# A graph network's gather loop: stores of gathered rows issued by ScalarE instead of SP

## The chip, the cores and the metric

One core of a Trainium2 chip. The metric is the time on the device of one execution, in microseconds (us). The kernel before takes 5740.17 us, the median of three runs (5734.01 to 5756.72).

## The reference, cut to what matters

Four layers of graph networks run one after the other on 6250 nodes of 128 features and 100,000 edges sorted by their target, each followed by a residual and a layer norm. The change lies in the second, a graph attention layer with four heads of 32:

```python
x_l = (x @ Wl + bl).reshape(n, H, C)
x_r = (x @ Wr + br).reshape(n, H, C)
e = (ea_f @ We).reshape(-1, H, C)
m = jax.nn.leaky_relu(x_l[src_f] + x_r[dst_f] + e, NEG_SLOPE)
alpha = jnp.einsum('ehc,hc->eh', m, att)
amax = jax.ops.segment_max(alpha, dst_f, num_segments=n)
aexp = jnp.exp(alpha - amax[dst_f])
asum = jax.ops.segment_sum(aexp, dst_f, num_segments=n)
alpha = aexp / (asum[dst_f] + 1e-16)
out = jax.ops.segment_sum(x_l[src_f] * alpha[..., None], dst_f, num_segments=n)
```

The sum over edges in the other layers is done as a product with a dense matrix of counts (adjacency) of 6272 x 6400 fp16 numbers, kept in HBM. The fourth layer needs that matrix transposed.

## The kernel before

The program is written for each engine by hand, with semaphores: every engine has its own list of instructions, which it does in order, and a wait holds up all that stands behind it on that engine. The stages are: building the matrix of counts by scattered writes, three dense layers, the attention layer (scores, maxima, sums), a dense layer pair, and a last pair that uses the transposed matrix.

**The stage of scores.** 832 visits (a visit is 128 edges of one tile of nodes) are done in 104 groups of U = 8, in 26 rounds of RING = 4. A group g uses slot j = g mod 4 of `msg`, a ring of four buffers of 128 x 8 x 128 fp32. What happens to a group:

- ScalarE (L771) copies its eight columns of indices into `stage`, once DVE has reported group g-4 as done (`s_add`). This sets off the gather.
- GpSimd (L624, "POOL") waits for the staging and issues eight indirect DMAs, one for each visit. Each gathers 128 rows of `x_l` from HBM into `msg`, and `s_gath[j]` counts what has landed.
- DVE (L1383) makes one-hot matrices one group ahead, PE (L966) transposes them, ScalarE (L773) copies the result to `diag`, and PE (L972) multiplies it with the rows of `x_r`.
- DVE (L1396 to L1406) waits for the products and for the gather, and computes the scores in six operations. Then it waits for the store of the same group (`s_store[j]`) and reports the group as done.
- SP (L518) waits for the gather and stores `msg[:, j]` to `gathered` in HBM, 512 KB, from where the stage of sums reads it back later.

**The transposes.** Beside this SP makes the transposed matrix of counts, in 25 rounds of four pieces. A piece is a DMA transpose (L515) from `adj` in HBM into a slot of `turns` in SBUF, and a save of it (L509, function `save`) into `turned` in HBM. `s_turn[j]` and `s_saved[j]` count both. In a round SP does, for each j: wait for the save of the round before, issue the transpose, wait for the gather of the group, issue its store, wait for the transpose, issue its save. The 26th round has stores alone (L523). DVE waits for all saves only after the stage, ahead of its scans, and the last layers read `turned`.

Of the kernel before, what the change touches and what calls it, by code (L numbers as in the profile page):

```python
# [16 lines left out]
P = 128  # L17
U = 8
RING = 4
# [18 lines left out]
def build(nc, x, src, dst, edge_weight, W1, b1, W2, b2, W3, b3, gWl, gbl, gWr, gbr, gWe, gatt, gbias,  # L38
# [5 lines left out]
    CT = TILES + 1  # L44
# [4 lines left out]
    ROUNDS = GROUPS // RING  # L49
# [18 lines left out]
    with ctx:  # L68
# [6 lines left out]
        def sem(name):  # L75
            return ctx.enter_context(nc.semaphore(name))

        def dram(name, shape, dt=F32):
            return nc.dram_tensor(name, shape, dt, kind="Internal").ap()
# [7 lines left out]
        gathered = dram("gathered", (VISITS // U * P, U * D))  # L87
# [110 lines left out]
        s_gath = [sem(f"s_gath{j}") for j in range(RING)]  # L198
        s_store = [sem(f"s_store{j}") for j in range(RING)]
# [81 lines left out]
        msg = rows_of[:, :, :, 0:D]  # L281
# [64 lines left out]
        def go(name):  # L346
            return GO.index(name) + 1
# [84 lines left out]
        def _(sp):  # L432
# [73 lines left out]
            def save(i, j):  # L506
                a, z = PARTS[j % 2]
                sp.wait_ge(s_turn[j], i * 16 + 16)
                sp.dma_start(turned[bass.ds(i * (2 * P) + j // 2 * P, P), a * P:z * P], turns[:, j, 0:(z - a) * P]).then_inc(s_saved[j], 16)  # L509

            with sp.Fori(0, CT // 2) as i:
                for j in range(RING):
                    a, z = PARTS[j % 2]
                    sp.wait_ge(s_saved[j], i * 16 + 16)
                    sp.dma_start_transpose(turns[:, j, 0:(z - a) * P].rearrange("p (o c) -> p o c", o=1),  # L515
                                           adj[a * P:z * P, bass.ds(i * (2 * P) + j // 2 * P, P)]).then_inc(s_turn[j], 16)
                    sp.wait_ge(s_gath[j], i * (16 * U) + 16 * U)
                    sp.dma_start(gathered[bass.ds(i * (RING * P) + j * P, P), :].rearrange("p (u f) -> p u f", u=U), msg[:, j, :, :]).then_inc(s_store[j], 16)  # L518
                    save(i, j)
            with sp.Fori(CT // 2, ROUNDS) as i:  # L520
                for j in range(RING):
                    sp.wait_ge(s_gath[j], i * (16 * U) + 16 * U)
                    sp.dma_start(gathered[bass.ds(i * (RING * P) + j * P, P), :].rearrange("p (u f) -> p u f", u=U), msg[:, j, :, :]).then_inc(s_store[j], 16)  # L523
            sp.wait_ge(s_go, go("shifted"))

            def read_back(a, z):
# [131 lines left out]
        def _(act):  # L658
# [108 lines left out]
            with act.Fori(0, ROUNDS) as i:  # L767
                for j in range(RING):

                    act.wait_ge(s_add, i * (RING * U) + (U * (j - RING + 1) + ADD0))  # L770
                    act.copy(stage[:, j * U:(j + 1) * U], idxA[:, bass.ds(i * (RING * U) + j * U, U)]).then_inc(s_staged, 1)  # L771
                    act.wait_ge(s_oT, i * RING + (j + 1))
                    act.copy(diag[:, j % 2, :, :], pm[:, j % 2, :].rearrange("p (u f) -> p u f", f=P)).then_inc(s_oTc, 1)  # L773
            act.wait_ge(s_go, go("shifted"))
            act.activation(ext[:, :, 0:H], ext[:, :, 0:H], ACT.Exp).then_inc(s_exp, 1)
            with act.Fori(0, ROUNDS) as i:
# [859 lines left out]
```

## Time and profile before

| | |
|---|---|
| median of the runs | 5740.17 us (5734.01 to 5756.72) |
| profiled execution | 5702.34 us |
| its span | 5700.5 us |
| busy in the span | PE 58%, DVE 49%, POOL 36%, ACT 29% |
| stage of scores | from about 2350 to 3640 us of the span |

The span is the time from the first to the last instruction of that one execution. Shares of busy time are means over stages with different limits. In the trace "SPq" and "ACTq" are the instructions with which an engine issues DMAs, and they do not count as its busy time; "issue" is idle time for which the profile shows no releaser, and "remote" idle time that ended on a semaphore whose sender it does not show.

### The profile page before, as it was taken

What the parts mean: (1) busy time and instruction counts of PE and PEld (TensorE: products, weight loads), DVE (VectorE), ACT (ScalarE), POOL (GpSimd) and SP (SyncE); (2) the same over time, 40 slices, a digit from 0 to 9 for tenths busy, and PEclk for the clock granted to TensorE, in tenths of its full rate; (3) what the DMA queues carried; (4) which work ended last, traced back from release to release, by engine and by line L of the source; (5) the groups of instructions that cost most, each with busy time, mean ns of one, the idle gap of its engine ahead of it and who ended that gap; (6) DMA issues with size and microseconds to landing.
All of it is one profiled execution on the core that took longest, in us unless ns stands there. A gap on an engine that the chain in (4) does not pass through costs nothing.

```text
span 5700.5 us, 61044 instructions
## 1 busy us (share of the span) xinstructions
PE 3324.1 (58%) x19159; PEld 3100.7 (54%) x19160; DVE 2808.7 (49%) x3801; ACT 1675.3 (29%) x2774; POOL 2048.7 (36%) x1982
## 2 busy tenths in 40 slices
PE   1300000019999999544444444357479999689697
PEld 0300000019999999544333343246379789589597
DVE  8300000024454544677666677788954344544345
ACT  0000000005645455200000000023266356456265
POOL 2777666750000000377677777346300000200300
PEclk9999999999999999755555555579789999799798
DMA  9700000008858587499899899247368268478585
GB/s 356 275 1 16 1 1 1 1 12 278 257 183 276 175 275 227 126 228 220 215 216 214 215 221 222 62 122 214 92 205 277 84 208 277 151 244 285 180 283 183
DMA packets 887483, 1008.44 MB, mean 177 GB/s; under 512 B 391651, under 2 KB 651705, under 8 KB 887270
## 3 DMA queue, kind: packets, MB, share of 16 engines
q1 hardware_dynamic: 795778, 861.50, 51.6%
q0 software_dynamic: 56208, 63.97, 4.8%
q10 hardware_dynamic: 35284, 80.30, 3.6%
q8 instruction: 113, 1.85, 0.1%
q14 instruction: 100, 0.82, 0.1%
HBM read 692.09 MB, written 233.14 MB: 162 GB/s over the span
## 4 chain that ended last, share of the span: by engine, by line
PE 44%; another core or an unknown queue 23%; DVE 14%; issue 11%; POOL 3%; ACT 2%; DMA 2%; DVEq 1%; SPq 0%; ACTq 0%; POOLq 0%
PE banks L918 35%; PE banks L841 4%; POOL work L624 2%; PE banks L1000 2%; DVE Z L1397 1%; DVE big L1519 1%; DVE Z L1402 1%; PE banks L863 1%; ACT banks L779 1%; DVE big L1406 1%; DMA work<-tab,stage 1%; DVE Z L1404 1%; ACT X L668 1%; PE banks L966 1%
## 5 line engine op out<-in xcount | busy, mean ns | idle before, releaser
L918 PE MATMUL banks<-wides,rows 128*128 128x384 f32 (+2 forms) x11040 | 2028.5, 344 | 155.8 <-issue 88.6
L918 PEld LDWEIGHTS banks<-wides,rows 128*128 128x128 f32 x11040 | 1949.4, 189 | 229.1 <-issue 94.3
L624 POOL DMA_INDIRECT work<-tab,stage x832 | 902.8, 1085 | 1483.0 <-ACT stage L771 1232.2
L1265 DVE CAST wides<-big 128x768 fp32r<-128x768 f16 (+3 forms) x1429 | 811.1, 569 | 1176.7 <-PE banks L918 1072.3
L698 ACT CAST wides<-big 128x768 fp32r<-128x768 f16 (+2 forms) x1037 | 832.2, 804 | 677.9 <-PE banks L918 554.3
L598 POOL DMA_INDIRECT cells<-queue_i x784 | 787.0, 1004 | 311.9 <-issue 298.6
L972 PE MATMUL banks<-V,work 128*128 x1664 | 372.5, 414 | 378.6 <-ACT work L773 312.1
L972 PEld LDWEIGHTS banks<-V,work 128*128 128x128 f32 x1664 | 345.1, 316 | 415.9 <-issue 415.9
L650 POOL DMA_INDIRECT V<-tab,nodei x100 | 96.2, 962 | 1201.9 <-DMA tab<-X 879.8
L863 PE MATMUL banks<-work 128*128 128x50 f16 x784 | 92.1, 278 | 670.6 <-issue 600.5
L863 PEld LDWEIGHTS banks<-work 128*128 128x128 f16 x784 | 73.1, 149 | 689.5 <-issue 612.6
L773 ACT COPY work<-banks 128x1024 f32<-128x1024 f32 x104 | 105.3, 1012 | 1152.4 <-remote 542.5
L696 ACT ACTIVATE wides<-big 128x768 fp32r<-128x768 f16 (+1 forms) x392 | 342.5, 874 | 186.4 <-PE banks L918 186.4
L966 PE MATMUL banks<-ident,work 128*128 128x128 f32 x832 | 184.5, 395 | 331.4 <-DVE work L1383 259.4
L661 ACT ACT_TABLE_LOAD x1 | 1.3, 1283 | 1250.5 <-DVEq L1053 1250.5
L1193 DVE TENSOR_TENSOR work<-big 128x400 f16<-128x400 f16 x98 | 36.2, 369 | 668.7 <-remote 641.0
L966 PEld LDWEIGHTS banks<-ident,work 128*128 128x128 f32 x832 | 148.5, 206 | 356.6 <-DVE work L1383 279.3
L1396 DVE TENSOR_TENSOR Z<-banks,work 128x1024 f32<-128x1024 f32 x104 | 127.1, 1222 | 310.5 <-remote 167.0
L1000 PE MATMUL banks<-work 128*128 128x137 f32 x1664 | 226.6, 289 | 84.8 <-ACT banks L779 53.6
L1000 PEld LDWEIGHTS banks<-work 128*128 128x128 f32 x1664 | 206.3, 193 | 105.3 <-issue 105.3
L639 POOL TENSOR_TENSOR work<-work,big 128x1024 f32<-128x1024 f32 x104 | 199.9, 1922 | 0.0
L779 ACT COPY banks<-zeros 128x1233 f32<-128x1233 f32 x104 | 123.6, 1189 | 176.6 <-DVE big L1519 176.6
(300 smaller groups left out, 3229.1 us busy)
## 6 DMA issues: line engine op xcount, KB each, us to landing
big<-cells SPq DMA_DIRECT2D x490, 416.0 KB
big<-cells SPq DMA_DIRECT2D x441, 384.0 KB
big<-turned SPq DMA_DIRECT2D x300, 384.0 KB
gathered<-work SPq DMA_DIRECT2D x104, 512.0 KB
work<-gathered SPq DMA_DIRECT2D x104, 512.0 KB, 4.2
big<-turned SPq DMA_DIRECT2D x100, 416.0 KB
cells<-work ACTq DMA_DIRECT2D x98, 416.0 KB, 14.6
turned<-big SPq DMA_DIRECT2D x50, 800.0 KB
```

The costliest lines, as they stand in the source:

```text
L598: pool.indirect_dma_start(cells[:, :], bass.IndirectOffsetOnAxis(ap=queue_i[:, b % 2, u:u + 1].bitcast(U32), axis=0), queue_i[:, b % 2, PI ...
L624: pool.indirect_dma_start(msg[:, j, u, :], None, tab[0][:, :], bass.IndirectOffsetOnAxis(ap=stage[:, j * U + u:j * U + u + 1].bitcast(U32) ...
L639: pool.tensor_tensor(m, m, by_head, ALU.mult).then_inc(s_msgs, 1)
L696: act.activation(to, of, ACT.Copy, accum_out=degs[:, s, k - OTHER + 1, w:w + 1]).then_inc(s_widea, 1)
L698: act.copy(to, of).then_inc(s_widea, 1)
L841: last = pe.matmul(pm[:, b % 2, i * P:(i + 1) * P], lhsT, rhs, start=(n == 0), stop=(n == len(ab) - 1))
L863: last = pe.matmul(col_ps, ohl[:, h, :, u], ohh[:, h, :, u], start=False, stop=False, skip_group_check=True)
L918: last = pe.matmul(banks[:, 4 * (w % 2) + j, 0:(z - a) * P], rows2[:, s, part * D:(part + 1) * D], wides[:, q % QUEUE, (a - start) * P:(z ...
L966: last = pe.transpose(pm[:, j % 2, u * P:(u + 1) * P], oh[:, j % 2, u, :], ident[:, :])
L972: last = pe.matmul(ps[:, j % 2, u, :], diag[:, j % 2, u, :], Vf[:, bass.ds(t * P, P)], start=True, stop=True)
L1000: last = pe.matmul(gsums[j % 2][:, bass.ds(slot, GW)], oh[:, j % 2, u, :], rows_of[:, j, u, :], start=False, stop=False, skip_group_check= ...
L1265: dve.tensor_copy(wides[:, (2 * m + 1) % QUEUE, 0:(z - a) * P], halves[:, m % HALVES, a * P:z * P]).then_inc(s_wided, 1)
```

## The change

ScalarE waits, after its copy to `diag`, for the gather of the same group and issues the store of its rows. In SP's loop the store and its wait are gone, and so is the loop for the 26th round. SP issues the transpose of piece j before it waits for transpose j-1 and saves it, so that two can be in flight; the last of a round is saved before the next round begins.

```diff
--- before.py
+++ after.py
@@ -514,13 +514,9 @@
                     sp.wait_ge(s_saved[j], i * 16 + 16)
                     sp.dma_start_transpose(turns[:, j, 0:(z - a) * P].rearrange("p (o c) -> p o c", o=1),
                                            adj[a * P:z * P, bass.ds(i * (2 * P) + j // 2 * P, P)]).then_inc(s_turn[j], 16)
-                    sp.wait_ge(s_gath[j], i * (16 * U) + 16 * U)
-                    sp.dma_start(gathered[bass.ds(i * (RING * P) + j * P, P), :].rearrange("p (u f) -> p u f", u=U), msg[:, j, :, :]).then_inc(s_store[j], 16)
-                    save(i, j)
-            with sp.Fori(CT // 2, ROUNDS) as i:
-                for j in range(RING):
-                    sp.wait_ge(s_gath[j], i * (16 * U) + 16 * U)
-                    sp.dma_start(gathered[bass.ds(i * (RING * P) + j * P, P), :].rearrange("p (u f) -> p u f", u=U), msg[:, j, :, :]).then_inc(s_store[j], 16)
+                    if j:
+                        save(i, j - 1)
+                save(i, RING - 1)
             sp.wait_ge(s_go, go("shifted"))
 
             def read_back(a, z):
@@ -771,6 +767,8 @@
                     act.copy(stage[:, j * U:(j + 1) * U], idxA[:, bass.ds(i * (RING * U) + j * U, U)]).then_inc(s_staged, 1)
                     act.wait_ge(s_oT, i * RING + (j + 1))
                     act.copy(diag[:, j % 2, :, :], pm[:, j % 2, :].rearrange("p (u f) -> p u f", f=P)).then_inc(s_oTc, 1)
+                    act.wait_ge(s_gath[j], i * (16 * U) + 16 * U)
+                    act.dma_start(gathered[bass.ds(i * (RING * P) + j * P, P), :].rearrange("p (u f) -> p u f", u=U), msg[:, j, :, :]).then_inc(s_store[j], 16)
             act.wait_ge(s_go, go("shifted"))
             act.activation(ext[:, :, 0:H], ext[:, :, 0:H], ACT.Exp).then_inc(s_exp, 1)
             with act.Fori(0, ROUNDS) as i:
```

ScalarE, in the loop of the stage of scores, before (the numbers of the lines are those of each kernel; `s_oT` is PE's transposes, `s_add` DVE's report):

```order
L771 ISA [waits s_add]
L771 COPY stage<-idxA 128x8
L772 ISA
L773 COPY work<-banks 128x1024 [waits s_oT]
L770 REGISTER_ALU
L771 ISA [waits s_add]
L771 COPY stage<-idxA 128x8
```

The same place in the changed kernel:

```order
L767 ISA [waits s_add]
L767 COPY stage<-idxA 128x8
L768 ISA
L769 COPY work<-banks 128x1024 [waits s_oT]
L770 ISA
L771 ISA [waits s_gath0]
L771 DMA gathered<-work 1024x1x128
L766 REGISTER_ALU
L767 ISA [waits s_add]
L767 COPY stage<-idxA 128x8
```

The wait for the gather and the store stand between the copy of one group and the staging of the next.

SP, the start of its loop in the same stage, before:

```order
L515 DMA_TRANSPOSE big<-cells 128x1x3200
L517 ISA
L518 ISA [waits s_gath0]
L518 DMA gathered<-work 1024x1x128
L509 ISA [waits s_turn0]
L509 DMA turned<-big 128x3200
L515 ISA [waits s_saved1]
L515 DMA_TRANSPOSE big<-cells 128x1x3072
```

And in the changed kernel:

```order
L515 DMA_TRANSPOSE big<-cells 128x1x3200
L515 ISA [waits s_saved1]
L515 DMA_TRANSPOSE big<-cells 128x1x3072
L509 ISA [waits s_turn0]
L509 DMA turned<-big 128x3200
L515 ISA [waits s_saved2]
L515 DMA_TRANSPOSE big<-cells 128x1x3200
```

The second transpose has moved ahead of the wait for the first, and nothing of the gathers is left.

## Rows read from the trace of the kernel before

**Rows 1.** The page: span, busy time of each engine, and the group of the gathers

```profile
span 5700.5 us, 61044 instructions
...
PE 3324.1 (58%) x19159; PEld 3100.7 (54%) x19160; DVE 2808.7 (49%) x3801; ACT 1675.3 (29%) x2774; POOL 2048.7 (36%) x1982
...
L624 POOL DMA_INDIRECT work<-tab,stage x832 | 902.8, 1085 | 1483.0 <-ACT stage L771 1232.2
```

**Rows 2.** Busy time by stretch: the stage of scores, and a piece near its end

```profile
core 0: us, PE busy (x) PEld busy (x) DVE busy (x) ACT busy (x) POOL busy (x), PEclk, DMA share, GB/s
2350.00:3640.00 1290.00, 564.61 (x2566) 501.37 (x2564) 896.14 (x740) 116.58 (x208) 902.76 (x832) 0.58 0.88 212
3590.00:3622.00 32.00, 18.18 (x81) 16.08 (x80) 29.27 (x26) 4.51 (x6) 25.33 (x22) 0.55 0.28 77
```

**Rows 3.** L624: durations (min/median/max), first and last start; what its idle time waited for

```profile
L624 POOL DMA_INDIRECT work<-tab,stage x832: 939/951/1996, 2350.4 to 3622.7; - x167
...
  issue: 250.8, 791
...
POOL work L624 <- ACT stage L771: 1232.2, 41, 1112.2
```

**Rows 4.** Lines of DMA issues: the store from SP, and ScalarE's clearing stores (ns min/median/max)

```profile
L518 SPq DMA_DIRECT2D gathered<-work x100: 453/578/715, 2383.7 to 3580.1; - x100
...
L740 ACTq DMA_DIRECT2D cells<-work x245: 5/867/3243, 22.9 to 282.4; - x123
```

**Rows 5.** Timeline of SP at the start of the stage: start, duration, instruction

```profile
2380.35 2.77 SPq L515 DMA_TRANSPOSE big<-cells  x1
...
2386.94 4.87 SPq L515 DMA_TRANSPOSE big<-cells  x1
...
2395.88 4.47 SPq L515 DMA_TRANSPOSE big<-cells  x1
...
2403.94 5.91 SPq L515 DMA_TRANSPOSE big<-cells  x1
```

**Rows 6.** Timeline of all engines, 3000 to 3031 us: three groups' last issues and landings

```profile
3000.73 0.94 POOL L624 DMA_INDIRECT work<-tab,stage  x1 [0.31 <-issue]
...
3005.95 0.58 SPq L518 DMA_DIRECT2D gathered<-work  x1
...
3008.91 5.36 SPq L515 DMA_TRANSPOSE big<-cells  x1
...
3011.59 0.96 POOL L624 DMA_INDIRECT work<-tab,stage  x1 [0.30 <-issue]
...
3015.33 1.01 ACT L773 COPY work<-banks 128x1024 f32<-128x1024 f32 x1 [21.44 <-remote]
...
3016.24 0.20 ACT L771 COPY stage<-idxA 128x8 int32 x1
...
3017.23 1.60 POOL L624 DMA_INDIRECT work<-tab,stage  x1 [4.68 <-ACT stage L771]
...
3019.22 0.59 SPq L518 DMA_DIRECT2D gathered<-work  x1
...
3020.64 6.16 SPq L515 DMA_TRANSPOSE big<-cells  x1
...
3028.15 0.95 POOL L624 DMA_INDIRECT work<-tab,stage  x1 [0.30 <-issue]
...
3031.08 0.57 SPq L518 DMA_DIRECT2D gathered<-work  x1
```

**Rows 7.** Timeline, the last gather of the stage

```profile
3622.68 1.33 POOL L624 DMA_INDIRECT work<-tab,stage  x1 [0.30 <-issue]
3626.25 0.53 SPq L523 DMA_DIRECT2D gathered<-work  x1
```

**Rows 8.** Waits in the stage: who waited for whom, us in total, times, longest

```profile
ACT work L773 <- remote: 542.5, 31, 22.1
...
ACT work L773 <- PE banks L966: 414.7, 50, 20.5
```

## The prediction, made before the changed kernel had run

> **What bounds the stage now.** The profile's page comes first [rows 1]: no engine is near its span, GpSimd's gathers (L624) carry 902.8 us in 832 instructions, and the line of that group names ScalarE's staging of indices (L771) as what ended its idle time. The stretch from 2350 to 3640 us is the stage of scores, the only one in which the edit changes an instruction [rows 2]: POOL 902.8 and DVE 896.1 of 1290 us, PE 565, ACT only 117, and the 16 DMA engines 0.88 busy. In the undisturbed end of the stage, without transposes, the DMA share is 0.28.
>
> The lines on L624 then split POOL's time [rows 3]. Its first issue is at 2350.4 us and its last at 3622.7, so 104 groups of eight issues take 1272.3 us, 12.23 us each. One issue is 1.085 us on average, and the idle time before one is some 0.30 us of "issue" (250.8 us in 791 cases). Of the 1232.2 us of waiting for ACT, 1112.2 are one wait before the stage, so 120.0 us in 40 cases lie inside it. A group is 8 x 1.085 + 7 x 0.305 = 10.8 us of issuing. So **POOL issues almost without a break now**: 10.8 of 12.2 us. It can do so because ScalarE stages the indices of a group ahead of time: it waits for group g-4 and for PE's transposes of group g, but never for the gather itself. DVE's 896.1 us are 8.6 us per group: it is not the bound.
>
> **What the change removes.** SP loses 104 store issues of some 0.58 us [rows 4] and 104 waits for gathers. Its transposes lose those waits too: now one transpose at a time is issued, and the next one only after a store of gathered rows. Nobody in this stage waits for a transpose or for its save; their results are first needed after the stage. This part is worth nothing by itself, unless the freed DMA time brings the gathers home earlier. It also makes the transposes come denser. The first four transposes of the stage, before SP had gathers to wait for, are issued at 2380.35, 2386.94, 2395.88 and 2403.94 us [rows 5], 7.9 us apart on average. I take 8.5 us, since the end of each loop turn waits for its last transpose with nothing else in flight: 100 of them take 850 us, not the 1200 of now.
>
> **What it adds, on the critical path.** ScalarE now runs, per group: wait for group g-4, stage g, wait for PE, copy the diagonal matrix of g, **wait until gather g has landed, issue its store**, and only then stage g+1. POOL cannot start gather g+1 before it is staged. What stands behind the new wait is therefore the one instruction that POOL depends on, and POOL's run-ahead is gone: the loop is POOL issues 8, the last one lands, ScalarE issues the store, ScalarE stages, POOL issues again. Its terms:
>
> - The issuing, 10.8 us as now. Below that, with every issue at its 0.951 us median [rows 3], 9.7 us.
> - From the end of the eighth issue to the start of the instruction that waits for the landing. I read it where SP waits in the same way today. Three groups in a row give 3001.67 to 3005.95 = 4.28, 3012.55 to 3019.22 = 6.67 and 3029.10 to 3031.08 = 1.98 us [rows 6]. SP's own transpose had been issued by 3014.27 in the second and 3026.80 in the third, so SP was waiting. Their mean is 4.3. Without transposes, at the end, it is 3624.01 to 3626.25 = 2.2 us [rows 7].
> - ScalarE's issue of the store. SP takes 0.578 us for it, and ScalarE 0.867 for one of its clearing stores [rows 4]. The first is the same transfer, so 0.6. Register work adds 0.1.
> - Start of staging to POOL's first issue: 3016.24 to 3017.23 = 1.0 us [rows 6].
>
> The sum is 10.8 + 4.3 + 0.7 + 1.0 = **16.8 us per group while transposes run**, and 10.8 + 2.2 + 0.7 + 1.0 = **14.7 us after them**. In the first 850 us fit 51 groups (857 us), and the other 53 take 779 us: 1636 us against 1272, **364 us more**.
>
> What else could be late: PE's work and ScalarE's copies hang on the staging of their group as before, and both together are (565 + 117) / 104 = 6.6 us per group [rows 2], which fits beside a gather of 15 us or more. DVE (896.1 / 104 = 8.6 us a group) finishes a group that long after its gather has landed, before the next one lands, so it falls idle instead. It waits for the store of its own group, which ScalarE issues at once and which has those 8.6 us to land. The next stages are not touched. They start later by the whole amount, since the scan waits for the last group.
>
> The profiled execution took 5702.3 us for a span of 5700.5. The sum would make it 6066. The median of the runs shown is 38 us above the profiled one, so the forecast for the median is 5740 + 364 = **6104 us**.
>
> The bounds of the terms together: 9.7 + 1.98 + 0.7 + 1.0 = 13.4 us per group gives 1394, or 5862 us; 10.8 + 6.7 + 1.0 + 1.0 = 19.5 gives 2028, or 6496 us. The landing is the open term. I take the mean of its rows for the first part and the undisturbed one for the rest, as the transposes end early.
>
> **Where a rule and the rows part.** The gathers' landing moves between 2.0 and 6.7 us with what SP has in flight [rows 6, 7]. The Trainium skill, "DMA: Bandwidth & Descriptors", section "SWDGE vs HWDGE vs iDMA", says that GpSimd's and SP's descriptors sit in different queues of each DMA engine and that the engine takes turns between them. By that rule a gather would wait for little of a transpose, and the landing would stay near its short value throughout. That is the first rival; the 6.67 us speak against it.
>
> **Rivals.**
>
> 1. Landings stay short under the transposes: 14.7 us in all 104 groups, 1529 us, **5997 us**. For it speaks the row of 1.98 us; against it 4.28 and 6.67. Chance 0.08. With the issuing faster as well, at the lower bound: 5862 us, chance 0.03.
> 2. The denser transposes hold up every gather as long as the worst row: 10.8 + 6.7 + 0.7 + 1.0 = 19.2 us for 850 us are 44 groups (845 us), and 60 of 14.7 are 882: 1727 us, **6195 us**. For it speaks that a transpose or a save would nearly always be in flight. Chance 0.12.
> 3. The DMA engines are the bound, and what they move per stage stays: no change, **5740 us**. For it stands the share of 0.88. Against it, POOL issues its gathers all the same, with 120 us of idle time in the stage. It would need DMA queues so full that a break of 6 us in every group costs nothing. Chance 0.03. The Trainium skill says in "DMA: Bandwidth & Descriptors", section "Issuing engines are not separate DMA queues", that starting DMAs from another engine saves only the time of issuing them: by this rule the gain side is nil, and the trace agrees as far as SP's issue of 0.58 us goes.
> 4. **Faster.** ScalarE arrives at the new wait when the gather has already landed. Then the wait is free, staging is as early as now, and the earlier landing of stores (no longer behind a transpose and its save in SP's order) takes away POOL's waits of 120.0 us: **5620 us**. This decides at the point where the diagonal copy (L773) starts after the landing. In the rows it starts at 3015.33, and the store of the same group goes out at 3019.22 [rows 6]; read in the same way over the timeline, the copy starts before the store in all but 2 of the 104 groups. For it speaks that ScalarE idles for PE before that copy (414.7 us) and for others (542.5 us) [rows 8], so it is late often, but not that late. Chance 0.04.
>
> That ScalarE would not wait in this order is excluded by the listing of its instructions.
>
> **Chances.** The forecast has 0.70. Slower by over 0.5% (29 us, about what a measurement of this kernel can tell) are the forecast and rivals 1 and 2: 0.70 + 0.08 + 0.03 + 0.12 = 0.93. Within it 0.03, faster 0.04. The range leaves out rivals 3 and 4 and the low bound (0.10) and the far ends of the landing: 5950 (14.2 us per group, between the two lower sums) to 6270 (17.3 us in every group, as if the transposes disturbed to the end).
>
> **What would show it.** In the profile of the changed kernel: POOL's idle time before L624 put down to ScalarE in nearly all 104 groups, 4 to 6 us each, some 500 us in all beside the wait before the stage; ScalarE's store 2 to 7 us after the eighth issue and its staging within 1 us of it; transposes 8 to 9 us apart and over by some 3250 us; DVE idle for gathers in every group; a lower DMA share, and POOL's pitch near 17 us early and 15 us late. It is wrong if POOL's issues still follow each other over the bounds of groups, or if the pitch does not fall once the transposes are over.

## The result: 5.7% slower, and the profile after

The changed kernel takes **6067.74 us** (median of four runs, 6065.19 to 6069.82) against 5737.82 us before: 330 us more, a ratio of 1.0566 with a 95% interval of 1.0545 to 1.0587. The forecast was 6104 us, in a range of 5950 to 6270.

The page of the changed kernel, in the rows that answer to [rows 1], and its DMA queues (number of packets, MB, share of 16 engines):

```profile
span 6067.3 us, 61052 instructions
...
L620 POOL DMA_INDIRECT work<-tab,stage x832 | 883.5, 1062 | 1876.7 <-ACT stage L767 1646.0
...
q1 hardware_dynamic: 687618, 806.96, 44.2%
q10 hardware_dynamic: 143444, 134.83, 6.5%
```

The gathers are L620 now. Their issuing takes what it took (883.5 us, 902.8 before), and the idle time ahead of them has grown. The stores have moved from SP's queue (q1) to ScalarE's (q10). The 832 issues, and the waits in the stage (who waited for whom: total us, times, longest):

```profile
L620 POOL DMA_INDIRECT work<-tab,stage x832: 940/952/1992, 2377.5 to 3991.6; - x167
...
POOL work L620 <- ACT stage L767: 1646.0, 104, 1145.2
ACT stage L767 <- DMA work<-tab,stage: 1093.7, 77, 19.4
...
DVE Z L1394 <- DMA work<-tab,stage: 644.4, 103, 11.6
```

The stage, from the first issue to the last, lasts 3991.6 - 2377.5 = 1614 us; before it was 1272 [rows 3]. POOL waits for ScalarE in all 104 groups: 1646.0 - 1145.2 = 500.8 us inside the stage, where it was 120.0 in 40 cases. ScalarE in turn waits for gathers to land, and so does DVE, for 644.4 us; before, the profile puts 109 us of DVE's idle time in the stage down to gathers, and 167 us to no sender that it shows. The transposes, which SP now issues alone, and the stage cut where they end (SP's line first, then busy time by stretch, with the columns of [rows 2]):

```profile
L515 SPq DMA_TRANSPOSE big<-cells x100: 1452/5430/8637, 2410.0 to 3102.7; - x100
```

```profile
2378.00:3130.00 752.00, 247.54 (x1094) 219.13 (x1092) 372.85 (x305) 48.79 (x87) 365.22 (x345) 0.56 1.11 278
3280.00:3990.00 710.00, 277.14 (x1194) 244.93 (x1192) 423.82 (x350) 55.44 (x100) 424.99 (x400) 0.58 0.26 74
```

They are 7.0 us apart ((3102.7 - 2410.0) / 99), and the last is issued at 3102.7 us. POOL makes 345 issues in 752 us while they run, which is **17.4 us per group**, and 400 in 710 us afterwards, **14.2 us per group**. The DMA share is 1.11 in the first part and 0.26 in the second. Two turns of the loop, in the timeline of the changed kernel (start, duration, instruction, idle time before it): one among transposes, then one after them.

```profile
2997.26 0.94 POOL L620 DMA_INDIRECT work<-tab,stage  x1 [0.30 <-issue]
...
3002.78 0.55 ACTq L771 DMA_DIRECT2D gathered<-work  x1
3003.74 0.20 ACT L767 COPY stage<-idxA 128x8 int32 x1 [15.99 <-issue]
...
3004.72 1.17 POOL L620 DMA_INDIRECT work<-tab,stage  x1 [6.53 <-ACT stage L767]
```

```profile
3806.68 0.94 POOL L620 DMA_INDIRECT work<-tab,stage  x1 [0.30 <-issue]
...
3809.52 0.55 ACTq L771 DMA_DIRECT2D gathered<-work  x1
3810.25 0.20 ACT L767 COPY stage<-idxA 128x8 int32 x1 [13.07 <-DMA work<-tab,stage]
...
3811.23 1.41 POOL L620 DMA_INDIRECT work<-tab,stage  x1 [3.61 <-ACT stage L767]
```

The chain can be read off: the eighth issue ends (2998.20), the gather lands and ScalarE issues the store (2.78, so 4.58 us later), then stages (0.96 later), then POOL issues again (0.98 later). In the second turn the first step takes 3807.62 to 3809.52 = 1.90 us, the other two 0.73 and 0.98. Averaged over groups, the first step takes 5.0 us in the first 43 and 1.7 in the others, and the other two together 1.8 in both. Nothing else of the program moved: from the last gather to the end of the span it is 2077.8 us before and 2075.7 after. The stage begins at 2350.4 us in the one profile and at 2377.5 in the other, with the same code ahead of it; in the first four experiments it begins anywhere from 2351 to 2368. So the spans lie 367 us apart, the stages 342 and the medians 330.

### The profile page after: what moved, and what is told of

The parts are those of the page before. It is cut to its first block, busy times and chain, and to the rows that moved or that the text cites. A ratio compares the mean times of both kernels' runs of the same rounds, so it can differ in the third digit from the quotient of the medians.

```text
span 6067.3 us, 61052 instructions
## 1 busy us (share of the span) xinstructions
PE 3338.1 (55%) x19159; PEld 3112.8 (51%) x19160; DVE 2813.1 (46%) x3801; ACT 1675.2 (28%) x2774; POOL 2014.3 (33%) x1982
## 4 chain that ended last, share of the span: by engine, by line
PE 40%; another core or an unknown queue 16%; POOL 12%; issue 11%; DVE 9%; DMA 7%; ACT 2%; ACTq 1%; DVEq 0%; SPq 0%; POOLq 0%
PE banks L916 32%; POOL work L620 12%; DMA work<-tab,stage 6%; PE banks L839 4%; PE banks L998 1%; ACTq L771 1%; DVE big L1517 1%; DVE Z L1302 1%; ACT banks L777 1%; PE banks L861 1%; ACT X L664 1%; DVE V L1113 1%; PE banks L826 0%; PE banks L892 0%
## 5 line engine op out<-in xcount | busy, mean ns | idle before, releaser
L620 POOL DMA_INDIRECT work<-tab,stage x832 | 883.5, 1062 | 1876.7 <-ACT stage L767 1646.0
L594 POOL DMA_INDIRECT cells<-queue_i x784 | 771.3, 984 | 320.2 <-issue 308.1
L767 ACT COPY stage<-idxA 128x8 int32 x104 | 20.5, 197 | 1480.8 <-DMA work<-tab,stage 1093.7
L1394 DVE TENSOR_TENSOR Z<-banks,work 128x1024 f32<-128x1024 f32 x104 | 127.4, 1225 | 650.2 <-DMA work<-tab,stage 644.4
## 6 DMA issues: line engine op xcount, KB each, us to landing
cells<-work ACTq DMA_DIRECT2D x98, 416.0 KB, 14.7
```

The source lines that it names most:

```text
L594: pool.indirect_dma_start(cells[:, :], bass.IndirectOffsetOnAxis(ap=queue_i[:, b % 2, u:u + 1].bitcast(U32), axis=0), queue_i[:, b % 2, PI ...
L620: pool.indirect_dma_start(msg[:, j, u, :], None, tab[0][:, :], bass.IndirectOffsetOnAxis(ap=stage[:, j * U + u:j * U + u + 1].bitcast(U32) ...
```

## The experiments

All ran as one core's program, each compared with the kernel before on the same chip. The experiments ran on three chips, of two sorts: on that of experiments 1 to 4 before takes 5711 us, about as above; on that of 5 to 8 and on that of 9 to 12, 5164 to 5165 us. Ratios hold within a chip; the lengths of the stage (first to last issue of the gathers) are set side by side where the same kernel ran on both.

### The wait, the store, the two halves

**1. The wait alone.** The kernel before, with ScalarE waiting for the gather, and SP storing and transposing as before:

```diff
                     act.copy(diag[:, j % 2, :, :], pm[:, j % 2, :].rearrange("p (u f) -> p u f", f=P)).then_inc(s_oTc, 1)
+                    act.wait_ge(s_gath[j], i * (16 * U) + 16 * U)
```

> The kernel before, with one added wait: ScalarE waits for the gather of group g before it stages group g+1. SP still issues stores and transposes as before. Theory (the wait takes away POOL's run-ahead): per group 10.7 us of issuing, 3.5 to 5 us to the landing, 1.1 us of staging, no 0.6 us store issue: 15.3 to 16.8 us, a stage of 1590 to 1750 us, a time of 6040 to 6200 us. Rival A (the store's 104 DMA issues on ScalarE are what costs): within 1% of before, 5680 to 5800 us. Rival B (the denser transposes hold up the gathers): within 1% of before too, since the transposes keep their old pace.

Measured: 5845.42 us, a ratio of 1.023 (1.0196 to 1.0264). The wait by itself costs 2.3%, so both rivals fall as sole causes, but the time lies 195 us under the low end of what I expected. The stage lasts 1409 us, 13.5 us per group:

```profile
L624 POOL DMA_INDIRECT work<-tab,stage x832: 942/947/1962, 2363.4 to 3772.3; - x167
```

```profile
2996.34 0.59 SPq L518 DMA_DIRECT2D gathered<-work  x1
...
2997.12 0.51 SPq L509 DMA_DIRECT2D turned<-big  x1
...
2997.76 6.57 SPq L515 DMA_TRANSPOSE big<-cells  x1
...
3006.42 0.95 POOL L624 DMA_INDIRECT work<-tab,stage  x1 [0.30 <-issue]
...
3009.10 0.20 ACT L771 COPY stage<-idxA 128x8 int32 x1 [11.66 <-DMA work<-tab,stage]
```

The rows (SP's store, save and transpose; POOL's eighth issue; ScalarE's staging) show why. SP issues its whole share right after a landing and has issued the transpose by 3004.33; the last gather of the next group goes out at 3006.42 and meets little of it. It lands 1.73 us after its issue (3007.37 to 3009.10). Where POOL stands still until a landing, and the transfers of SP start at the same landing, the two keep out of each other's way. I had taken the landing from a kernel in which they do not.

**2. The store one group late.** The changed kernel, with ScalarE's wait and store for group g-1 behind the copy of group g (`store` is the same wait and store for a given group; round 0 is written out, since its first group has none in front):

```diff
-                    act.wait_ge(s_gath[j], i * (16 * U) + 16 * U)
-                    act.dma_start(gathered[bass.ds(i * (RING * P) + j * P, P), :].rearrange("p (u f) -> p u f", u=U), msg[:, j, :, :]).then_inc(s_store[j], 16)
+                    if j:
+                        store(i * (16 * U) + 16 * U, bass.ds(i * (RING * P) + (j - 1) * P, P), j - 1)
+                    else:
+                        store(i * (16 * U), bass.ds(i * (RING * P) - P, P), RING - 1)
```

> The changed kernel, with ScalarE's wait and store moved one group later: stage g, copy g, then wait for gather g-1 and store it. SP as changed (dense transposes, no stores). Theory: staging of g+1 waits only for the landing of g-1, which falls into POOL's issuing of g, so POOL issues without a break: 11.0 to 12.2 us per group, stage 1150 to 1270 us, time 5610 to 5740 us. Rival A (store issues on ScalarE cost): stays above 5950 us, for there are as many. Rival B (dense transposes cost): stays well above before in the first 700 us of the stage, a pitch of 15 us or more there. Rival C (the 16 DMA engines are the bound, at 0.88 busy before): no faster than before, 5700 to 5780 us, with DMA share near 1.

Measured: 5728.52 us, 1.0031 (1.0013 to 1.0049). ScalarE issues as many stores, SP's transposes run free as well (8.0 us apart), and nearly the whole loss is gone. So neither the number of stores on ScalarE nor the dense transposes cost much by themselves; they cost where POOL waits for what stands behind them. Busy time while the transposes run and after them:

```profile
2400.00:3190.00 790.00, 355.70 (x1520) 313.64 (x1520) 531.81 (x444) 73.37 (x127) 567.07 (x509) 0.57 1.17 281
3220.00:3640.00 420.00, 185.69 (x856) 164.57 (x855) 296.29 (x246) 41.08 (x70) 300.11 (x279) 0.60 0.32 88
```

509 issues in 790 us are 12.4 us per group, against 17.4 in the changed kernel under the same DMA share of 1.1 to 1.2. The hoped-for gain did not come: POOL still makes only 279 issues in the 420 us after the transposes, 12.0 us per group. The waits in that kernel's stage name one place:

```profile
DVE work L1398 <- DMA gathered<-work: 168.1, 54, 8.6
```

DVE waits for the store of its own group, which now goes out a group late. It is the smaller part, though: read group by group, POOL's 35 waits in the stage come to 124 us, and 77 us of them (19 waits) follow a copy to `diag` that PE's transposes held up, as in the kernel before on this sort of chip (experiment 9).

**3. One transpose in flight.** The changed kernel, with SP saving each transpose before it issues the next:

```diff
-                    if j:
-                        save(i, j - 1)
-                save(i, RING - 1)
+                    save(i, j)
```

> The changed kernel, but SP saves each transpose before it issues the next, so one is in flight. Theory: the loop over ScalarE stays, transposes come some 9 to 10 us apart instead of 7.0 and disturb more groups each a little less: 6040 to 6110 us, within 1% of the changed kernel. Rival B (density is what costs): falls by 150 us or more, to below 5920 us. Rival A: as the changed kernel.

Measured: 6063.26 us, 1.0632 (1.0582 to 1.0681), a stage of 1629 us. This is what the theory expected. Stretches with and without transposes:

```profile
2385.00:3330.00 945.00, 315.25 (x1352) 277.68 (x1352) 477.91 (x395) 63.21 (x114) 475.65 (x449) 0.56 0.96 230
3345.00:3970.00 625.00, 244.71 (x1054) 214.99 (x1052) 370.60 (x307) 47.69 (x86) 373.61 (x352) 0.55 0.26 73
```

16.8 us per group for 945 us, then 14.2 for the rest: less disturbance for longer. The changed kernel did not run on this chip; against its stage on the two others (1614 and 1609 us), one transpose in flight or two makes little difference. That they run free of the gathers does (experiment 5).

**4. The new order of SP alone.** The kernel before, with SP's stores kept and its saves one piece late:

```diff
-                    save(i, j)
+                    if j:
+                        save(i, j - 1)
+                save(i, RING - 1)
```

> The kernel before, with the second half of the change alone: SP keeps the stores and their waits, but issues transpose j before it waits for and saves transpose j-1. Theory: the transposes stay paced by the gathers they wait for (one to a group), ScalarE runs ahead as before: 5700 to 5770 us. Rival B (two transposes in flight hold up the gathers): slower than before by over 1%, above 5800 us. Rival A: as before.

Measured: 5705.02 us, 0.998 (0.9957 to 1.0003): no difference. This half of the change costs and gives nothing while SP waits for a gather between two transposes.

### What the free transposes cost, and the waits moved

**5. Transposes tied to the gathers.** The changed kernel, with SP waiting for the gather of a group before it saves:

```diff
             def save(i, j):
                 a, z = PARTS[j % 2]
+                sp.wait_ge(s_gath[j], i * (16 * U) + 16 * U)
```

> The changed kernel, with one more wait on SP: each save of a transpose waits for the gather of its group, so that one save and one transpose follow each landing, as in the first experiment. ScalarE waits and stores as changed. Theory after the first four runs: the cost has three parts, the wait (135 us, where landings stayed at 2.1 us), the store issue of 0.6 us between landing and staging, and transposes that run free of the gathers' rhythm and so meet the last gather of a group (5.0 us to the landing instead of 1.7 in the first 43 groups). Tied, the third part goes: 14.2 us per group throughout, a stage of 1470 to 1510 us, 3.5 to 4.3% above before. Rival (it is the stores on ScalarE's own DMA queue that meet the gathers, not the free transposes): stays at 5.3% or more above before.

**8. The changed kernel on the same chip.** 

> The changed kernel once more, on the same chip as the fifth to seventh experiments, for comparison: 5.4 to 6.2% above before.

Measured: 5521.41 us tied, 1.0688 (1.067 to 1.0706), and 5635.03 us for the changed kernel, 1.0918 (1.0899 to 1.0937). In ratios both expectations failed, for on this chip the kernel before is faster than on that of experiments 1 to 4, from which they were made; the length of the tied kernel's stage, expected at 1470 to 1510 us, held. The gathers of the tied kernel, and then those of the changed kernel:

```profile
L621 POOL DMA_INDIRECT work<-tab,stage x832: 940/953/6997, 2039.2 to 3539.1; - x167
```

```profile
L620 POOL DMA_INDIRECT work<-tab,stage x832: 940/953/7009, 2035.0 to 3644.0; - x167
```

Tied 1500 us, changed 1609 us (1614 on the first chip). Tying the transposes gives 109 us back, with the stores still on ScalarE's queue. The landings say the same: from the end of the eighth issue to the store, averaged over all groups but the last few, 1.9 us tied, and 4.6 us in the changed kernel's first 44 groups on this chip. The rival, stores on their own queue, falls. Tied transposes also come less densely, 14.1 us apart and not 7.1, but density alone does not explain the short landings: in the kernel before on the first sort of chip they are 12.0 us apart and SP's store starts 4.3 us after the last issue while they run; in experiment 1 they are 13.3 us apart, and it starts after 1.9 us.

**6, 10 and 12. DVE's wait for the store moved.** The kernel before, where DVE no longer waits for the store of its group; ScalarE does, before it stages the group four later (`staging` is its wait for DVE and its copy of indices; round 0 is written out, and DVE waits once for all stores after the loop):

```diff
-                    dve.wait_ge(s_store[j], i * 16 + 16)
                     dve.sem_inc(s_add, U)
...
+                    act.wait_ge(s_store[j], i * 16)
                     staging(i * (RING * U) + (U * (j - RING + 1) + ADD0), bass.ds(i * (RING * U) + j * U, U), j)
```

> The kernel before, with DVE's wait for the store of its own group moved to ScalarE, which needs that store only before it stages the group four later. SP as before. Theory (before, POOL's 120 us of waits come from DVE held up by stores that queue behind transposes): POOL issues without a break, 11.1 us per group, a stage of 1150 to 1200 us, 1.2 to 2.1% below before. Rival C (the DMA engines are the bound): within 0.5% of before.

> DVE's wait for the store moved to ScalarE, again. Where before takes some 5700 us and POOL waits 120 us in the stage: POOL issues without a break, 10.9 to 11.2 us per group, 1.5 to 2.4% below before. Rival C (the DMA engines are the bound on such a chip): 12.2 us per group, within 0.5%. Where before takes 5165 us: within 0.3% of it, as in the sixth experiment.

> DVE's wait for the store moved to ScalarE, a third time, since both runs so far came from chips where before takes 5165 us and issues its gathers without a break already. Where before takes some 5700 us: if its 12.2 us per group come from DVE held up by late stores, 10.9 to 11.3 us per group and 1.5 to 2.4% below before; if from the chip's own pace of transfers (rival), 12.2 us and within 0.5%. Where before takes 5165 us: within 0.3%, and the question stays open.

Measured: 5159.45 us, 0.9987 (0.9978 to 0.9997), then 5158.89 us, 0.999 (0.9981 to 0.9999), and 5160.25 us, 1.0001 (0.999 to 1.0012). All three runs fell on chips where before takes some 5165 us, and there this wait costs next to nothing, so no run settles the question it was made for, what the 120 us of POOL's waits come from on the first sort of chip. The traces of the kernel before answer a part of it (experiment 9).

**7. Both.** Experiment 2 with the same move.

> The second experiment (ScalarE stores one group late, SP's transposes free) with the same move of DVE's wait. Theory: both parts of the wait are off the path, 11.1 to 11.6 us per group, a stage of 1150 to 1210 us, 1 to 2% below before. Rival C: within 0.5% of before. If it is slower than the sixth experiment, the free transposes cost something even where POOL runs ahead.

Measured: 5172.49 us, 1.0016 (1.0006 to 1.0026), no gain. But its stage is 1153 us, 11.1 us per group, with free transposes 8.9 us apart, and a gather's last packet ends 5.3 us after its last issue while they run, later even than in the changed kernel (3.8 us on this chip). A late landing costs POOL next to nothing where the staging does not wait for it.

### The kernel before, on the other chips

**9. The kernel before.**

> The kernel before, unchanged, for its trace on the same chip as the two runs beside it. The runs of the fifth to eighth experiments came from a chip where before takes 5165 us and the changed kernel 470 us more, not 330. Theory: the stage of the changed kernel is the same on both (1614 and 1609 us), and that of before is not: it should be near 12.2 us per group where before takes 5700 us, and near POOL's own 11 us per group (1140 us) where it takes 5165 us.

Measured: 5161.21 us, 0.9995 (0.9983 to 1.0006). Its gathers, its waits, and its busy time in the stage:

```profile
L624 POOL DMA_INDIRECT work<-tab,stage x832: 941/950/7005, 2036.8 to 3178.0; - x167
...
ACT work L773 <- PE banks L966: 1020.0, 104, 17.8
POOL work L624 <- ACT stage L771: 819.4, 8, 815.5
...
POOL work L624 <- issue: 251.2, 824, 0.3
```

```profile
2040.00:3170.00 1130.00, 584.34 (x2503) 515.82 (x2502) 875.73 (x720) 114.28 (x206) 877.72 (x823) 0.59 0.98 240
```

The same instructions take 1141 us here, 11.0 per group, instead of 1272. POOL waits for ScalarE 819.4 - 815.5 = 4 us in the stage, not 120, and nothing but issuing is left, although SP's store starts only 6.4 us after the last issue on average. So the changed kernel loses 9.2% on such a chip (experiment 8) and 5.7% on the first sort, although it takes the same time in the stage: the run-ahead that it gives up was worth more where it worked without a hitch. The DMA share is 0.98.

The hitch can be seen in the two traces of the kernel before. Here ScalarE's copy to `diag` (L773) always starts within 0.1 us of the end of PE's transposes (L966). On the chip of the result that wait ended 31 times on a semaphore whose sender the profile does not show [rows 8], and in as many groups the copy starts more than 1 us, and up to 10.9 us, after the end that the profile gives for the transposes:

```profile
3003.03 1.97 PE L966 MATMUL banks<-ident,work 128*128 128x128 f32 x8 [5.22 <-issue]
```

Those eight transposes end at 3005.00 us, and the copy starts at 3015.33 [rows 6]; the staging stands behind it and is late, and POOL waits 4.68 us. Of POOL's 26 waits of over 0.5 us in that stage, 119 us in all, 25 with 107 us stand behind such a copy. In the changed kernel and in experiment 1, where POOL pauses in every group, no copy is held up by PE. The same shows far ahead of the stage, in a loop in which DVE and PE wait for each other in turn to count edges, on the page of the kernel before there:

```profile
L1193 DVE TENSOR_TENSOR work<-big 128x400 f16<-128x400 f16 x98 | 36.2, 369 | 668.7 <-remote 641.0
```

In all six traces from the first sort of chip DVE waits there 30 to 42 times for over 15 us each, and in none of the eight from the other sort. Why PE's results come late on those chips is not known: PE's ends in a profile are modelled, so it does not say whether PE worked longer or its report came late.

**11. No transposes.** The kernel before without the transposes and their saves; the last layers read the untransposed matrix.

> The kernel before without the transposes and their saves (the last layers read the untransposed matrix, so the results of the fourth network are others, with transfers of the same size). Theory: landings of 1.6 to 2.2 us throughout and no held-up stores, 10.9 to 11.2 us per group, a stage of 1130 to 1165 us: 1.5 to 2.4% below before where before takes 5700 us, within 0.5% where it takes 5165 us. Rival (POOL's pitch of 12.2 us comes from the chip's own pace of gathers): 12.2 us per group without transposes too.

Measured: 5156.48 us, 0.9983 (0.9971 to 0.9996). Busy time in the stage:

```profile
2040.00:3170.00 1130.00, 576.44 (x2496) 509.00 (x2496) 886.71 (x728) 116.48 (x208) 871.07 (x827) 0.58 0.36 99
```

The stage goes from 1141 to 1130 us, while the DMA share falls from 0.98 to 0.36. The transposes are hidden in the kernel before, and the DMA engines are not its bound on this chip.

## Why the prediction was right

**The mechanism** is shown by two runs, one that adds the wait to the kernel before and one that moves it, with its store, in the changed kernel. Put ahead of the staging (1), it costs 2.3% in the kernel before; moved behind the next copy together with its store (2), it leaves 0.3% of a loss of 5.7%. POOL's idle time was forecast at some 500 us beside the wait before the stage, and is 500.8.

**The terms.** Issuing stayed at 10.7 to 10.8 us. Store to staging to POOL's issue was forecast at 1.7 and took 1.8 us on average. The undisturbed landing was put at 2.2 us and is 1.7, which gave 14.2 instead of 14.7 us per group. Among transposes I took 4.3 us; the mean over the 43 groups is 5.0, which gave 17.4 instead of 16.8. The transposes came 7.0 us apart, not 8.5, so that 43 groups met them and not 51. The three errors pull in two ways (some 26 us more, and 30 and 17 less): a stage of 1614 us against 1636. That they nearly cancel is luck. Set against 1272, that is 342 where I had 364. The other 12 us, from the stages' 342 to the medians' 330, lie in what single executions differ by: the profiled one of before was 35 us below the median of its runs, and the sum was made against it.

**What the sum did not separate.** It put the whole loss down to the wait and the order behind it. The runs divide it in three steps, in us per group: 12.2 before; 13.5 with the wait alone (1); 14.4 with the store's issue between landing and staging as well (5); 15.5 with the transposes set free (the change). The third of these was measured on the other sort of chip, where before takes 11.0 and the changed kernel 15.5 as well; that the steps add up over both sorts is taken from the changed kernel's equal stage. The first step is 1.3 us only because POOL already waits 1.2 us per group (120 us in 104 groups) in the kernel before. The last step came into my sum only through the landing that I had read from the kernel before, and experiment 1 shows that this reading was not justified: with the wait added and nothing else, landings get short. It fitted the changed kernel because there SP runs free, for another reason than in the kernel before.

**The rivals.** Short landings throughout (rival 1, the rule of queues served in turn) did not come: the landing is 4.6 to 5.0 us while transposes run, 1.7 to 1.8 without, so a queue of its own does not keep a gather clear of them. Of rival 2, the denser transposes, there was a part: 5.0 us on average and up to 10.2, but not 6.7 throughout. Rival 3 is refuted for the change: the stage's DMA share reached 1.11 and fell to 0.26, with the pitch at 17.4 and 14.2 us, never at the old one. Rival 4 needed ScalarE to arrive later than the landing; it waited for the gather, as DVE did, nearly every time. Its gain, POOL's waits of 120 us gone by earlier stores, was misread too: those waits stand behind late results of PE (experiment 9), not behind stores.

**Open.** Before takes 12.2 us per group on the chips of the result and of experiments 1 to 4, and 11.0 on the others. The traces put POOL's part of this down to late results of PE; why they are late there is open, and no run changes it. The packets of a transpose and of a store take about the same on both (medians of 4.0 and 3.7 us, and of 2.0 and 1.9), and the wait that I suspected could be tried only where it does no harm.

## What to carry to other kernels

A DMA moved to an idle engine brings its wait along, and all that the engine was doing ahead of time then stands behind that wait. Look for who needs the next instruction: here a 0.2 us copy of indices fed the engine that sets the pace. If the DMA has to go there, put it one step late, behind the work of the next round; that took back nearly all of the loss.

## What was unexpected

- A wait can shorten a transfer. With the wait alone, SP's store started 2.1 us after the last issue on average, not 4.4. The likely reason, which experiment 5 supports, is that SP's transfers then begin at the same moment as POOL's pause. The wait cost 1.3 us per group over the kernel before, and not the 3.1 to 4.6 that I expected.
- The same program takes 5711 and 5165 us on different chips, and the loss from one edit is 5.7% on one and 9.2% on another. The stage of the changed kernel is the same on both within 5 us (1614 and 1609); that of the kernel before differs by 131 (1272 and 1141). Most of the 540 us between the chips lies outside the stage: the profiled span is 314 us longer ahead of it and 95 us behind it.
